# Last stage of a two-layer kernel: subtraction moved to VectorE, eviction to ScalarE, residual added by accumulating GpSimd transfers

## What is computed

```python
x = x + _L0_ffn_ref(_L0_cond_ref(x, ...), ...)      # layer 0: conditioned mix, gated feed-forward
x = x + _L1_ffn_ref(_L1_cond_ref(x, ...), weight)   # layer 1: grouped convolution, 8-bit product
```

```python
x_scale = FP8_MAX / max(|x|);  w_scale = FP8_MAX / max(|weight|)
x_fp8 = clip(x * x_scale, -448, 448) rounded to fp8;  w_fp8 likewise
out = (x_fp8 @ w_fp8) * (1.0 / x_scale * (1.0 / w_scale))
```

## Time and profile before

| | us |
|---|---|
| median of 3 runs (lowest to highest) | 440.19 (439.18 to 440.75) |
| span of the profiled execution, first to last instruction | 438.0 |

### The profile page before, as it was taken

One profiled execution on the slowest core, in us unless ns is written; L12 is line 12 of the kernel. 1 busy time (PEld: TensorE's weight loads), 2 busy tenths in 40 slices (PEclk: granted clock), 3 DMA queues, 4 the chain that ended last, 5 costly groups with the idle time before them and its releaser, 6 DMA issues.

```text
span 438.0 us, 5261 instructions
## 1 busy us (share of the span) xinstructions
PE 408.8 (93%) x1981; PEld 322.3 (74%) x1981; DVE 264.6 (60%) x395; ACT 176.3 (40%) x289; POOL 132.1 (30%) x91
## 2 busy tenths in 40 slices
PE   8889999999999999999999999989999999982654
PEld 7737887778888867888887788878779999980211
DVE  1748877636476643647666254878934434448994
ACT  3627656313466541336665124557622211124210
POOL 3660332423133331422523052233220411002660
PEclk9659999999999999999999999999999999995896
DMA  7903464242101000210100024001065444700234
GB/s 238 353 4 96 149 225 121 73 167 97 48 1 49 0 1 0 97 49 1 48 2 0 1 96 144 1 5 44 1 175 149 119 138 142 216 25 0 94 123 168
DMA packets 32409, 37.90 MB, mean 87 GB/s; under 512 B 2168, under 2 KB 19576, under 8 KB 32256
## 3 DMA queue, kind: packets, MB, share of 16 engines
q1 hardware_dynamic: 32384, 37.57, 25.9%
HBM read 24.98 MB, written 12.58 MB: 86 GB/s over the span
## 4 chain that ended last, share of the span: by engine, by line
PE 87%; DVE 8%; ACT 2%; issue 2%; DVEq 0%
PE ps L521 37%; PE ps L505 19%; PE ps L548 10%; PE ps L503 5%; PE ps L527 5%; PE ps L465 3%; PE ps L583 2%; DVE m L1143 2%; DVE o_buf L1134 2%; PE ps L636 1%; PE ps L427 1%; PE ps L453 1%; DVE x_lo L886 1%; PE ps L552 1%; PE ps L479 1%
## 5 line engine op out<-in xcount | busy, mean ns | idle before, releaser
L821 POOL TENSOR_TENSOR h_lo<-a_buf,h_hi 128x512 fp32r<-128x512 f32 (+1 forms) x44 | 58.6, 1331 | 143.2 <-ACT h_hi L717 143.2
L521 PE MATMUL ps<-x_hi,gate_w 128*128 128x512 f32 (+1 forms) x176 | 70.4, 400 | 0.0
L521 PE MATMUL ps<-x_lo,gate_w 128*128 128x512 f32 (+1 forms) x176 | 70.2, 399 | 0.0
L521 PE MATMUL ps<-x_hi,up_w 128*128 128x512 f32 (+1 forms) x176 | 69.6, 395 | 0.0
L505 PE MATMUL ps<-down_w,h_hi 128*128 128x512 f32 (+1 forms) x176 | 69.4, 394 | 0.0
L505 PE MATMUL ps<-down_w,h_lo 128*128 128x512 f32 (+1 forms) x176 | 69.4, 394 | 0.0
L521 PE MATMUL ps<-x_lo,up_w 128*128 128x512 f32 (+1 forms) x176 | 69.3, 394 | 0.0
L1049 DVE TENSOR_TENSOR a_buf<-a_buf,b_buf 128x512 f32<-128x512 f32 (+1 forms) x44 | 53.4, 1213 | 13.7 <-ACT a_buf L762 12.3
L1046 DVE TENSOR_TENSOR b_buf<-ps,b_buf 128x512 f32<-128x512 f32 (+1 forms) x44 | 30.3, 688 | 24.7 <-ACT b_buf L751 19.5
L751 ACT ACTIVATE b_buf<-ps,up_sc 128x512 f32<-128x512 f32 (+1 forms) x44 | 30.2, 686 | 31.5 <-PE ps L521 31.4
L748 ACT ACTIVATE a_buf<-ps,gate_sc 128x512 f32<-128x512 f32 (+1 forms) x44 | 30.2, 686 | 29.4 <-POOL h_lo L821 27.3
(11 more groups left out here) (151 smaller groups left out, 621.1 us busy)
## 6 DMA issues: line engine op xcount, KB each, us to landing
turned<-stage SPq DMA_DIRECT2D x16, 512.0 KB, 3.0
x_nat<-in_x SPq DMA_DIRECT2D x4, 1024.0 KB, 7.2
xt<-turned SPq DMA_DIRECT2D x8, 512.0 KB, 4.5
out<-o_buf SPq DMA_DIRECT2D x7, 512.0 KB, 2.8
x_nat<-in_down_q SPq DMA_DIRECT2D x11, 256.0 KB, 3.0
x_nat<-in_gate_q SPq DMA_DIRECT2D x10, 256.0 KB, 4.9
x_nat<-in_up_q SPq DMA_DIRECT2D x10, 256.0 KB, 5.0
x_hi<-turned SPq DMA_DIRECT2D x4, 512.0 KB, 4.0
```

The source lines that it names most:

```text
L521: last = mm(ps[0:k, bank(ic, 2 * m), :], w[:, H * ic + c * k:H * ic + (c + 1) * k], part[:, c, :], start=c == 0 and part is x1_hi, stop=c ...
L821: nc.gpsimd.tensor_tensor(h_lo[0:k, ic, :], a_buf[0:k, ic % 2, :], plain(h_hi[0:k, ic, :]), ALU.subtract).then_inc(h_lo_ready, 1)
```

## The change

- Step 4 is on VectorE for all nine steps. GpSimd computes nothing in the stage.
- Step 7 is on ScalarE and only evicts: `o_buf = psum * out_scale`. x2 is not added there.
- x2 of each group is written to `out` by SyncE right behind `store(g)` (`fill(g)`, 256 KB, 16 of them).
- The product is added to `out` in DRAM by GpSimd transfers with `accum_op=add`, one per step. Before the first, GpSimd waits until all 16 fills have landed.
- o_buf has four slots in place of two (`OUTS = 4`), with a semaphore each; the product uses all four pairs of PSUM banks.
- VectorE's order in an iteration n becomes v_plus(n), clip(n-1), m(n+1), subtract(n). ScalarE's becomes output(n-3), magnitude(n).

```diff
+OUTS = 4
+            def fill(g):
+                sp.wait_ge(x2_ready, g + 1)
+                sp.dma_start(out[g * P:(g + 1) * P, :], x_nat[:, g, :]).then_inc(filled, 16)
...
                 store(g)
+                fill(g)
...
                 if j < TG - 1:
                     store((TILES - 1) * TG + j)
+                    fill((TILES - 1) * TG + j)
+            fill(GROUPS - 1)
-            for n, (g, k) in enumerate(steps):
-                sp.wait_ge(o_ready, n + 1)
-                sp.dma_start(out[...], o_buf[:, n % 2, ...]).then_inc(out_done[n % 2], 16)
...
 # TensorE
-                if n >= 2:
-                    pe.wait_ge(o_ready, n - 1)
+                if n >= 4:
+                    pe.wait_ge(o_ready, n - 3)
...
 # ScalarE
+            def output(n, k):
+                act.wait_ge(ffn_mm, n + 1)
+                if n >= OUTS:
+                    act.wait_ge(out_done[n % OUTS], 16 * (n // OUTS))
+                activation(o_buf[:, n % OUTS, ...], out_banks(n, k), copy, scale=out_scale).then_inc(o_ready, 1)
+            act.wait_ge(x_scale_ready, 1)
+            for n, (g, k) in enumerate(steps):
+                if n == 3:
+                    act.wait_ge(x_scale_ready, 4)
+                if n >= 3:
+                    output(n - 3, steps[n - 3][1])
+                magnitude(n, g, k)          # waits for m(n-2), as before
+            for n in range(len(steps) - 3, len(steps)):
+                output(n, steps[n][1])
...
 # GpSimd
-                nc.gpsimd.tensor_tensor(q_raw[...], v_plus[...], m16[...], ALU.subtract)
+            pool.wait_ge(filled, 16 * GROUPS)
+            for n, (g, k) in enumerate(steps):
+                pool.wait_ge(o_ready, n + 1)
+                nc.gpsimd.dma_start(out_rows(g, k), o_buf[:, n % OUTS, ...],
+                                    accum_op=ALU.add).then_inc(out_done[n % OUTS], 16)
...
 # VectorE
+            round_from(0, *steps[0])                 # m(0)
+            for n, step in enumerate(steps):
+                add_round(n, *step)                  # v_plus(n)
+                if n > 0:
+                    clip(n - 1, *steps[n - 1])
+                if n + 1 < len(steps):
+                    round_from(n + 1, *steps[n + 1]) # m(n+1)
+                subtract(n, *step)
+            clip(n, *steps[n])
```

More of the change, by code:

```diff
@@ L176, in build @@
         q_fp8 = sb("q_fp8", [P, 2, 2 * H], BF16, phase2)
-        o_buf = sb("o_buf", [P, 2, 2 * H], F32, phase2)
+        o_buf = sb("o_buf", [P, OUTS, 2 * H], F32, phase2)
         phase2.close()
@@ L205, in build @@
         ffn_in = sem("ffn_in")
-        out_done = [sem(f"out_done{n}") for n in range(2)]
+        out_done = [sem(f"out_done{n}") for n in range(OUTS)]
+        filled = sem("filled")
         const_set = sem("const_set")
@@ L268, in build @@
         v_plus_ready = sem("v_plus_ready")
-        q_raw_ready, q_own_ready = sem("q_raw_ready"), sem("q_own_ready")
+        q_raw_ready = sem("q_raw_ready")
         q_fp8_ready = sem("q_fp8_ready")
@@ L316, in conv_out, with out_banks, out_rows @@
             return banks[:, :, part, :]
+        def out_banks(n, k):
+            return ps[:, 2 * (n % 4):2 * (n % 4) + k, :]
+        def out_rows(g, k):
+            return out[g * P:(g + k) * P, :].rearrange("(k p) h -> p k h", p=P)
         def plain(ap):
@@ L412, in _ @@
                     store((TILES - 1) * TG + j)
-            for n, (g, k) in enumerate(steps):
-                sp.wait_ge(o_ready, n + 1)
[L415 to L418, removed]
+                    fill((TILES - 1) * TG + j)
+            fill(GROUPS - 1)
+            for n in range(OUTS):
+                sp.wait_ge(out_done[n], 16 * len(range(n, len(steps), OUTS)))
         @block.tensor
@@ L631, in _ @@
                 pe.wait_ge(q_fp8_ready, n + 1)
-                if n >= 2:
-                    pe.wait_ge(o_ready, n - 1)
+                if n >= 4:
+                    pe.wait_ge(o_ready, n - 3)
                 for j in range(k):
                     for c in range(HC):
-                        last = mm(ps[:, 2 * (n % 2) + j, :], by_chunk(q_fp8[:, n % 2], k)[:, c, j * P:(j + 1) * P],
+                        last = mm(out_banks(n, k)[:, j, :], by_chunk(q_fp8[:, n % 2], k)[:, c, j * P:(j + 1) * P],
                                   ffn_q[:, c * H:(c + 1) * H], start=c == 0, stop=c == HC - 1)
@@ L789, in _, with magnitude @@
                             conv_low(g)
-            act.wait_ge(x_scale_ready, 1)
-            for n, (g, k) in enumerate(steps):
+            def magnitude(n, g, k):
                 if n >= 2:
@@ L796, in _ @@
                            scale=x_round).then_inc(v_ready, 1)
+            def output(n, k):
+                act.wait_ge(ffn_mm, n + 1)
+                if n >= OUTS:
+                    act.wait_ge(out_done[n % OUTS], 16 * (n // OUTS))
+                activation(o_buf[:, n % OUTS, 0:k * H].rearrange("p (k h) -> p k h", k=k), out_banks(n, k), copy,
+                           scale=out_scale).then_inc(o_ready, 1)
+            act.wait_ge(x_scale_ready, 1)
[7 more added lines that the diff above has]
+                output(n, steps[n][1])
         @block.gpsimd
@@ L831, in _ @@
                         stage_low(n)
+            pool.wait_ge(filled, 16 * GROUPS)
             for n, (g, k) in enumerate(steps):
[L834 to L840, removed]
+                pool.wait_ge(o_ready, n + 1)
+                nc.gpsimd.dma_start(out_rows(g, k), o_buf[:, n % OUTS, 0:k * H].rearrange("p (k h) -> p k h", k=k),
+                                    accum_op=ALU.add).then_inc(out_done[n % OUTS], 16)
         @block.vector
@@ L1106, in _, with round_from, add_round, subtract @@
                             ALU.mult).then_inc(x_scale_ready, 1)
-            def subtract(n, k):
+            def round_from(n, g, k):
+                dve.wait_ge(v_ready, n + 1)
+                v.tensor_scalar(m16[:, n % 2, 0:k * H], v16[:, n % 2, 0:k * H], ROUND_MIN, None,
+                                ALU.max).then_inc(m_ready, 1)
+            def add_round(n, g, k):
+                dve.wait_ge(m_ready, n + 1)
+                v.scalar_tensor_tensor(by_chunk(v_plus[:, n % 2], k), t_t[:, :, g * P:(g + k) * P], x_scale,
+                                       by_chunk(m16[:, n % 2], k), ALU.mult, ALU.add).then_inc(v_plus_ready, 1)
+            def subtract(n, g, k):
                 dve.wait_ge(v_plus_ready, n + 1)
                 v.tensor_tensor(q_raw[:, n % 2, 0:k * H], v_plus[:, n % 2, 0:k * H], m16[:, n % 2, 0:k * H],
[L1112 to L1121, removed]
+                                ALU.subtract).then_inc(q_raw_ready, 1)
+            def clip(n, g, k):
+                dve.wait_ge(q_raw_ready, n + 1)
                 if n >= 2:
@@ L1125, in clip @@
                                 ALU.min, ALU.max).then_inc(q_fp8_ready, 1)
[L1127 to L1158, removed]
+            round_from(0, *steps[0])
[7 more added lines that the diff above has]
+            clip(n, *steps[n])
 def kernel(x, cond_128, fside_S_0, L0_cond_W0, L0_cond_b0, L0_cond_W1, L0_cond_b1, L0_cond_W2, L0_cond_b2,
```

## The result

The changed kernel takes 455.29 us (median of 4 runs, 454.6 to 456.61) against 439.69 (4 runs, 438.5 to 440.75). The ratio is 1.0382, with a 95% interval of 1.0345 to 1.0419. The profiled execution took 455.52 us with a span of 453.5. That is outside the range given (437.5 to 446.0), on the side that held 0.41 of the chance, and next to the 453.9 of one rival's serial form.

What follows compares the result with a forecast made beforehand. VectorE set the pace before; afterwards a loop through ScalarE was to bound the steps at 3.65 us. -2.2 us at the last output and +2.7 at the end gave +0.5: span 438.5, time 440.7, range 437.5 to 446.0.

Steps and rivals of the forecast that it cites:

- one rival's serial form: Last stage: each accumulating transfer must land before the next is issued, 5.8 us each, 453.9 us; within a rival of chance 0.18.
- the one on the end: After the last output: one last transfer adds 2.7 us to 3.2; descriptor writing in earlier steps is hidden by o_buf's slots.
- a case with 0.18: Last stage: accumulating transfers set the pace, 443.4 us at 4.3 us each or 453.9 if serial; chance 0.18.
- The prediction's sign for this rival: Last stage: ScalarE waiting for a transfer ahead of output would show that the transfers set the pace.
- VectorE and the loop: Last stage: VectorE's own sum 3.02 us a pair, the loop through ScalarE 3.65 a step; last output 2.2 us earlier.
- No POOL busy time: Last stage: a sign that the forecast's steps are right would be no busy time on GpSimd (POOL).
- The last transfer: End of kernel: GpSimd's issue 1.3 us and the data 1.4, together +2.7 us.
- the upper bound: End of kernel: issue 2.24 us plus a read like a separate 256 KB load, 3.0, together 5.2 us.
- The fills: SP's queue: sixteen 256 KB writes cost nothing; without the cover of SP's early loads, 1.1 us once.
- both rivals: TensorE's clock: stays up to the end, 438.7 us, chance 0.22; or falls in mid-stage, 442.4 to 444.1, chance 0.15.
- GpSimd's issuing against VectorE: Last stage: GpSimd's issuing stops VectorE's m and clip, 0.74 us a step, 443.3 to 445.9 us; chance 0.08.

Runs made afterwards that it cites:

- the plain writes: The changed kernel with its 1024-byte ring and plain writes in place of the accumulating ones, so the output lacks x2: 437.19 us, ratio 0.9963.
- the halves: The changed kernel with its 1024-byte ring and each pair's product added by two 256 KB transfers in place of one of 512 KB: 445.75 us, ratio 1.0157.
- the larger ring: The changed kernel with 4096 bytes per partition in place of 1024 for the descriptors of GpSimd's transfers: 440.97 us, ratio 1.0061.
- Undoing the loop: The changed kernel with a 4096-byte ring and ScalarE's output(n-4) in place of output(n-3) ahead of magnitude(n): 435.69 us, ratio 0.9931.
- the compute part alone: The changed kernel without fills or adding: SyncE writes the product plainly from the four slots, x2 is left out: 436.01 us, ratio 0.9945.
- the fastest version: 4096-byte ring, output(n-4), and the last three steps evicted on VectorE with x2 added and written plainly by SyncE, without fills: 431.98 us, ratio 0.9848.

## Why the prediction was wrong, step by step

- **The step that failed** is the one on the end. It adds one last transfer behind the last output and holds the work of the steps before to be hidden, because a slot of o_buf is used again only 14.6 us later. It looked at o_buf's slots and not at GpSimd's own queue. Each accumulating pair was held until the one before had landed, 6.2 us a pair, and 19.8 us followed the last output where 5.9 were taken (3.2 + 2.7). With a ring that takes two, the kernel falls from 1.0382 to 1.0061, so the hold cost 3.2%, 14.1 us. That this is ring space is shown by the ring's size alone, by the plain writes, and by the halves; how many entries each kind takes is worked out, not seen.
- **The rival was there and was underpriced in chance.** The serial form, 5.8 us a pair and 453.9, is what happened at 6.2 and 455.3. It stood at the edge of a case with 0.18, and the range left it out. What spoke against it was the DMA share, twice 0.37 and so below one. That says nothing about how many transfers may be under way. It was also too low: the adding took 2.7 times the engines' time, not twice, and the 0.6 seen here is low only because of the hold. With the larger ring it reaches 0.96 near the end. The prediction's sign for this rival came true: at 433.01 ScalarE waits 4.28 us for a transfer ahead of an output.
- **VectorE and the loop**: right. 3.0 and 4.3 us in turn, clip(7) 29.6 us into the stage for 29.8. Undoing the loop gives steps of 3.00, VectorE's own sum. That the compute part alone came out 2.4 us faster for 2.2 is luck in part, since in its profile the clock fell in mid-stage and was full at the end. "No POOL busy time" was wrong as a sign, since the profile counts the issues as busy (1.2 us each).
- **The last transfer**: mechanism right, size too small. With the larger ring it adds 7.7 - 3.2 = 4.5 us behind the last output; 2.7 was taken and 5.2 the bound. By the ratios, adding costs 1.0061 - 0.9963 = 1.0%, 4.3 us (3.8 by the medians), over plain writes from GpSimd. A single group takes 5.3 to 5.5 us to land, 2.9 to 3.1 more than the 2.4 before, like the separate load of the upper bound (3.0). Without the hold the forecast of 440.7 stands beside 440.97, but by luck in part: the kernel before was 438.6 in that comparison, so the real step was +0.6%, not +0.1%.
- **The fills**: free, as taken.
- **The clock**: both rivals occur. In the changed kernel's profile the last twelve matmuls take 2.77, not 4.82; in the compute part alone the clock falls in mid-stage. Neither matters to the changed kernel, whose end is set by the transfers.

```profile
425.67 2.77 PE L629 MATMUL ps<-agg_b,q_fp 128*128 128x512 bf16 x12 [1.27 <-DVE q_fp L1139]
```

- **GpSimd's issuing against VectorE**: wrong as a rival. One m beside an issue takes 0.55 (404.07, with an issue from 403.65), 0.13 more than 0.42, not 0.74. The other two of VectorE's m and clips on pairs that ran beside an issue, from 409.07 and 414.75, took 0.43 and 0.42.

## What to carry to other kernels

Before work is moved to a queue, ask how much room its items take, how many can be under way and what holds the next one; here a share of 0.6 with an idle issuer was the sign that something other than the transfer engines was full. Idle time put down to "issue" ahead of a transfer means that none of the program's waits holds it. Where an in-order engine is given an eviction, put it far enough behind the work that feeds the chain: one more step of distance was worth 1.3% here. Adding in the transfer took 2.3 to 2.7 times the transfer engines' time of plain writes (25.2 us with the faster steps, 29.4 in the changed kernel, against 11.0), so look at the backlog it leaves behind the compute part: the fastest version does not add the last three steps that way.

## What the runs showed of the hardware

- Adding into DRAM: 512 KB land in 5.9 to 6.0 us against 3.2 plainly from the same queue, and in 6.7 to 6.9 behind a backlog. At a full share 199 GB/s of result moved over 8 us, and plain writes reached 262 over 2 us at a share of 0.69.
- GpSimd takes 1.2 us to issue 512 KB with the adding, and 0.72 without:

```profile
408.02 0.72 POOL L847 DMA_DIRECT2D out<-o_buf  x1 [3.95 <-ACT o_buf L796]
```

- A ring of 1024 bytes per partition holds the issues of accumulating pairs to one per 6.2 us, and of halves of pairs to two per 4.5 us; plain pairs aren't held. 2048 bytes don't hold accumulating pairs at all.
